# A fused attention and expert block on one core: three moves in the order of work on VectorE and ScalarE

## What is computed

```python
h = _layernorm(x) * (1 + ca) + sa
x = x + ga * attention(h)      # q, k = silu(h Wq), silu(h Wk); v, u = h Wv, h Wu
                               # kv_new = decay * kv + (k * k_decay)^T v, carried over the blocks
                               # o = q kv + masked (q k^T) v;  y = u * rms_normalised(o);  y Wout
h = _layernorm(x) * (1 + cb) + sb
out = (silu(h Wg_s^T) * (h Wu_s^T)) Wd_s^T               # shared expert
for e in range(8):
    out += (silu(h Wg[e]^T) * (h Wu[e]^T)) Wd[e]^T * comb[:, e]   # top 2 of 8
x = x + gb * out
```

## Time and profile before

| | us |
|---|---|
| median of the runs | 389.35 (389.18 to 389.91) |
| the profiled execution's own time | 391.22 |
| its span in the profile | 389.4 |
| busy PE / PE weight loads / DVE / ACT / POOL | 370.2 / 317.9 / 279.9 / 217.2 / 193.2 |
| mean granted clock of TensorE | 0.991 |

### The profile page before, as it was taken

How to read it: one execution, slowest core, us unless ns; L and a number is a source line. 1 busy time by engine, 2 the same in 40 slices (tenths; PEclk the granted TensorE clock), 3 DMA queues, 4 the chain that set the end, 5 groups by cost and what they waited for, 6 DMA issues and landing times.

```text
span 389.4 us, 12937 instructions
## 1 busy us (share of the span) xinstructions
PE 370.2 (95%) x4983; PEld 317.9 (82%) x4983; DVE 279.9 (72%) x561; ACT 217.2 (56%) x453; POOL 193.2 (50%) x193
## 2 busy tenths in 40 slices
PE   8989998999999888999995999999999999999996
PEld 4545555778877768899985999999999999999995
DVE  6986487898888786579983767758677785656553
ACT  5688676677667644648354655554646553433322
POOL 2000005787768665311373357686766665664340
PEclk9999999899999999999998999999999999999999
DMA  8952040000295006999432348564686776574543
GB/s 267 355 73 39 0 161 3 2 4 29 75 337 133 29 22 220 342 341 260 101 93 71 89 87 85 109 112 83 107 101 89 120 85 107 101 106 80 78 56 109
DMA packets 53043, 45.35 MB, mean 116 GB/s; under 512 B 31524, under 2 KB 46996, under 8 KB 52856
## 3 DMA queue, kind: packets, MB, share of 16 engines
q1 hardware_dynamic: 43048, 32.09, 29.9%
q0 software_dynamic: 7488, 10.27, 19.2%
q10 hardware_dynamic: 2448, 2.18, 1.8%
HBM read 27.60 MB, written 10.49 MB: 98 GB/s over the span
## 4 chain that ended last, share of the span: by engine, by line
PE 66%; POOL 12%; DVE 10%; issue 7%; ACT 3%; ACTq 0%; DVEq 0%; POOLq 0%
PE ps L1629 33%; PE ps L1647 16%; PE ps L1412 7%; POOL tmp L554 2%; POOL tmp L575 2%; POOL tmp L558 2%; POOL tmp L573 2%; POOL wx L563 2%; POOL h2s L579 2%; PE ps L1340 2%; DVE tmp L1253 1%; PE ps L1398 1%; PE ps L1532 1%; DVE tmp L1259 1%; PE ps L1509 1%
## 5 line engine op out<-in xcount | busy, mean ns | idle before, releaser
L1629 PE MATMUL ps<-tmp,wx 128*128 128x128 bf16 x1776 | 107.3, 220 | 5.2 <-ACT tmp L818 4.9
L1629 PEld LDWEIGHTS ps<-tmp,wx 128*128 (+1 forms) x1776 | 103.6, 99 | 6.5 <-ACT tmp L818 5.2
L611 POOL DMA_INDIRECT out<-tmp,dk x39 | 66.5, 1706 | 47.3 <-SPq L515 42.3
L856 ACT ACTIVATE tmp<-tmp 128x512 bf16<-128x512 f32 x55 | 34.6, 630 | 84.9 <-PE ps L1647 48.7
L1647 PE MATMUL ps<-wx,tmp 128*128 (+1 forms) x660 | 80.8, 273 | 0.3 <-DVE tmp L1259 0.2
L1253 DVE TENSOR_TENSOR tmp<-ps,tmp 128x512 f32<-128x512 f32 x55 | 37.9, 690 | 47.9 <-PE ps L1629 38.9
L1647 PEld LDWEIGHTS ps<-wx,tmp 128*128 128x128 bf16 x660 | 62.0, 98 | 7.8 <-issue 0.8
L1629 PE MATMUL ps<-w_hl,wx 128*128 128x128 bf16 x864 | 51.5, 219 | 1.0 <-ACT tmp L845 0.9
L1629 PEld LDWEIGHTS ps<-w_hl,wx 128*128 (+1 forms) x864 | 49.7, 98 | 1.7 <-issue 1.3
L606 POOL DMA_INDIRECT tmp<-h2rows,src_i x39 | 40.8, 1046 | 17.2 <-issue 10.7
L1259 DVE TENSOR_TENSOR tmp<-tmp 128x512 bf16<-128x512 f32 x55 | 37.8, 687 | 11.3 <-ACT tmp L856 10.8
(11 more groups left out here) (194 smaller groups left out, 569.1 us busy)
## 6 DMA issues: line engine op xcount, KB each, us to landing
wx<-in_wexp SPq DMA_DIRECT2D x26, 512.0 KB, 5.1
xres<-in_x SPq DMA_DIRECT2D x4, 512.0 KB, 7.2
h2rows<-h2s ACTq DMA_DIRECT2D x16, 128.0 KB, 4.0
out<-h2s SPq DMA_DIRECT2D x12, 128.0 KB
h2s<-in_wmod SPq DMA_DIRECT2D x1, 1024.0 KB, 9.4
wx<-decay_rows SPq DMA_DIRECT2D x16, 64.0 KB
modr<-mod_rows SPq DMA_DIRECT2D x1, 1024.0 KB, 4.7
wx<-in_wqkvu SPq DMA_DIRECT2D x1, 768.0 KB, 7.4
```

What stands on the lines that cost most here:

```text
L611: e.indirect_dma_start(t["out"], bass.IndirectOffsetOnAxis(ap=dst_i[:, j:j + 1], axis=0), yb[(NA + j) % 2], None, compute_op=ALU.add).then ...
L856: e.activation(hs[p][:, 0:FF], hf[p], ACT.Copy).then_inc(s["inner_high"], 1)
L1629: ins = e.matmul(half(bank, m * P), weight(at_, weights(part, w) + k * FF + m * P, P), xT[f % NXT][:, (2 * a + k) * P:(2 * a + k + 1) * P] ...
```

## The change

Three pieces of code stand in another place; nothing is added or taken away. In ACT's `middle(11)` the eviction `take_rows(12)` stands ahead of `split_high(1, 0)`. In DVE's prologue the low part of the weights' chunk 3 stands behind the moments of groups 2 and 3. In each attention step DVE makes the new state ahead of gating y.

```diff
@@ ACT, middle(f)
                     if f == EXP_AT:
                         softmax()
+                    if f == NA - 1:
+                        take_rows(NA)
                     for piece in PIECES_AT.get(f, ()):
                         split_high(*piece)
-                    if f == NA - 1:
-                        take_rows(NA)
                     wait(e, "inner_made", f + 1)
@@ DVE, prologue
             normalise(1)
-            weights_low(3)
             moments(2)
             moments(3)
+            weights_low(3)
             inputs_low(1)
@@ DVE, step_attention(n)
                 if mine(n) and n:
                     decay_scores(n)
-                if mine(v):
-                    _, b, i, j = tile_of(v)
-                    wait(e, "values_added", v + 1)
-                    wait(e, "squares", v + 1)
-                    wait(e, "out_product", v - 1)
-                    e.tensor_tensor(yfeat[:, v % 2], half(O_BANK, 0, D).rearrange("p (k n) -> p k n", k=KD),
-                                    ufeat[i // 2][:, i % 2, :, j * P:(j + 1) * P], ALU.mult).then_inc(s["y_gated"], 1)
                 if mine(n, NSTATE):
                     b = n % B
                     new = half(KT_BANK, D, D).rearrange("p (k n) -> p k n", k=KD)
                     wait(e, "kv_product", n + 1)
                     if n < B:
                         e.tensor_copy(state[:, b], new).then_inc(s["state_made"], 1)
                     else:
                         wait(e, "state_masked", n - 1)
                         wait(e, "state_decayed", KD * (n - 1))
                         e.tensor_tensor(state[:, b], state[:, b], new, ALU.add).then_inc(s["state_made"], 1)
+                if mine(v):
+                    _, b, i, j = tile_of(v)
+                    wait(e, "values_added", v + 1)
+                    wait(e, "squares", v + 1)
+                    wait(e, "out_product", v - 1)
+                    e.tensor_tensor(yfeat[:, v % 2], half(O_BANK, 0, D).rearrange("p (k n) -> p k n", k=KD),
+                                    ufeat[i // 2][:, i % 2, :, j * P:(j + 1) * P], ALU.mult).then_inc(s["y_gated"], 1)
```

## The result

| | median | runs | |
|---|---|---|---|
| before, same chip | 389.31 us | 4 (389.18 to 389.91) | |
| after | 381.12 us | 4 (380.34 to 381.49) | ratio 0.9781, 95% interval 0.9767 to 0.9796 |

The ratio times 389.3 is a gain of 8.5 us, with an interval of 7.9 to 9.1, and a time of 380.8 us beside the 389.35 that the prediction started from. The forecast was 382.1, the range 380.9 to 384.1: the gain is 1.2 us larger than forecast, and the time lies just under the range. The profiled execution of after took 380.34 us and has a span of 378.5; PE is busy for 364.9 us of it (96%).

A forecast was written before the change was run, and what follows sets the result against it. The prediction took PE, the busiest engine, as the bound, with its longest single wait at tile 12. Terms -6.46 - 0.5 - 0.33 = -7.3 us took the median from 389.35 to 382.1 us, range 380.9 to 384.1.

The forecast's parts named there:

- part 1, the hole: Tile 12: with the eviction ahead of the cast, PE starts at 203.44 instead of 208.48, gaining 5.04 us.
- part 1, the clock behind it: Tile 12: without the hole its 48 matmuls take 2.84 us instead of 4.26, gaining 1.42 us.
- part 2: Prologue: moving DVE's subtraction behind the moments lets ACT's root L666 start sooner, gaining 0.5 us.
- part 3, step 1: Attention step 1: PE's wait for the copy L1104 shortens, gaining 0.33 us once.
- part 3, steady steps: Twelve steady attention steps: idle time of 0.30 us moves from ahead of L1074 to ahead of L1080; gain 0.
- the two covers of 0.7 and 0.9 us: After tile 12's earlier start: room before PE waits for the third low part (0.7) and tile 11's low part (0.9).
- once more 1.4: Price if the clock stays low or falls elsewhere: again a half clock's cost here, 1.4 us, giving 383.5.
- the matmuls' low clock behind step 1's hole: Attention step 1: one of two reasons given for a time under 381.5, together given a chance of 0.03.
- The rival on the falling clock: Prologue's new hole or tile 12: the clock falls elsewhere or stays low, giving 383.5; chance 0.12.
- The prologue's new hole: Prologue, about 21.3 us: PE waits 0.95 us for the moved subtraction, covered by 1.14 us of existing idle time.
- the ring: Steady attention step: L1115, L773, L737 and L1080 wait on each other, setting 5.29 us whatever the swapped order.

The follow-up runs named there:

- e7: The kernel before, unchanged, run again for a second trace and twelve more times: 388.95 us, ratio 0.9991 against before.
- e13: The kernel before with 80 useless matmuls on PE ahead of the gate of tile 12, on a quiet chip: 387.19 us, ratio 0.9944.
- e5: The kernel before with 24 useless matmuls at the end of attention step 1 on PE, on a noisy chip: 391.27 us, ratio 0.9944.
- e9: The changed kernel with ACT's root L737 issued one place earlier, ahead of L773: 376.26 us, ratio 0.9656 against before.
- e2: The kernel before with only DVE's low part of chunk 3 moved behind the moments: 388.54 us, ratio 0.9972.
- e3: The kernel before with only DVE's new state moved ahead of gating y in the attention steps: 387.95 us, ratio 0.9955.
- e1: The kernel before with only ACT's eviction moved ahead of the cast: 382.46 us, ratio 0.9817.

## Why the prediction was right in kind and short in size

| step | predicted | found | from |
|---|---|---|---|
| part 1, the hole | -5.04 | -5.0 | starts of tile 12 in e7 and after: 206.37 - 200.82, less 0.56 of head start |
| part 1, the clock behind it | -1.42 | -2.2 | mean of four traces; e13 2.2 (1.4 to 3.0) |
| part 2 | -0.5 | -0.33 | PE's first attention rows, after against e7 (0.4 over all traces) |
| part 3, step 1 | -0.33 | -0.24 | 0.33 less 0.1 that L1080's wait gives back |
| part 3, clock of step 1 | not in the sum | -0.8, worked out | 16 of 28 executions x 1.35 us |
| part 3, steady steps | 0 | 0 | 80.87 us over the row of L1080s in before and after |
| sum | -7.3 | -8.6 | measured -8.5 (-9.1 to -7.9) |

**Part 1** stood as argued: the eviction needs only the turned rows and ACT's turn, PE's hole went whole, the two covers of 0.7 and 0.9 us held, and ACT and DVE caught up in two tiles. The first step that failed is "The 48 matmuls took 4.26 us there and 2.84 at 213.88: 1.42 us lost". It took a single execution's loss for the loss; the runs put it at 2.2 us. That execution was the cheapest of the four traced, one episode where the others had two: 1.42 against 2.11, 2.40 and 2.77, the hole being the same. The bound that I gave a half clock, "once more 1.4", was for the rivals upwards; nothing in the range stood for the clock costing more before, and so gaining more now.

**Step 1's clock** is the second step that failed, a term that the sum put at nothing: "the matmuls' low clock behind step 1's hole" was in the 0.03 for less than 381.5, and some 0.8 us in its place is what traces and counts give. The row that would have priced it, 0.57 in 68 to 72 us, was in the trace, next to rows 6. The mean clock told of it too, where the prediction took its 0.991 as a sign against a swinging clock: 0.009 of 389.4 us is 3.5 us of clock missing, tile 12's window holds 0.34 x 4.3 = 1.5 of them, and 68 to 72 us holds 0.43 x 4.0 = 1.7. I priced the clock where the wait table showed its longest entry, and did not go down the clock column over the whole span. The two clock terms are 0.8 us each above what I had; parts 2 and 3 gave 0.26 less. That makes 1.3 us, against 1.2 missing. That the shorter hole ends the episodes rests on counts, 16 of 28 against 0 of 20, and on e5, where useless work in the same hole did the same.

**The rival on the falling clock** had it at the wrong place and with the wrong sign. The prologue's new hole of 1.07 us cost no clock: it is in after, whose nine executions all have 0.999 or 1.0. The Trainium skill, "TensorE: Matmul & The Clock Gate", section "A second HAM failure mode: psum-queue depth-cycling", which I held against this change, has many small idle times make the clock swing. In this kernel the clock fell in the attention's first steps in some executions before the change, behind one hole of 1.90 us, and no longer did with the hole at 1.57; whether what the page tells of is at work here no run shows. Its outcome here, 383.5, did not come.

**Part 2** was read rightly in place and hole, and is a little smaller than 0.5. Its run alone gave 0.7 to 1.5, more than the move of 0.3 to 0.4 us that the traces show; a part of that is the baseline (against the 36 executions it is 0.7), the rest is clock, or open.

**Part 3** at nothing in the steady steps is the best supported of all: 80.87 us over the row of L1080s in before and in after, the plain step of 5.29 in every trace of that order, and e9, in which the wait ahead of L1080 goes as soon as the ring is opened. A plain step falls by no more than 0.08 us there, since PE comes next; the three steps with a cast inside the ring show it more plainly, 18.69 to 14.33. The cover of this zero was what the prediction named, L1115 and L773 and L737 and L1080 in a ring.

**The sum's baseline.** The profiled execution of before took 391.22 us, more than any of the 56 later ones of that kernel on the quiet chips (at most 390.33). Its span is 10.9 us longer than that of after, of which 1.8 us are in the routed tiles (from tile 13 at 213.88 to an L1647 at 370.10, 156.2 us, where e7 takes 154.4, from 213.12 to 367.50), only 0.5 of them shown as idle time of PE, and 0.94 the start-up, which differs between executions of any of these kernels (the first warm-up matmuls, L1340, take 5.38 us in e7, 5.68 in e2, 6.79 in e3 and 6.83 in e1). Taking its difference from the median off, as the prediction did, kept both out of the sum. What made the routed tiles slower is open.

## What to carry to other kernels

Price a hole of PE with the clock behind it, and take that price from several executions: the mean clock of each run counts the low stretches even where there is one trace. Check that the parts, run alone, add up to the whole; here they made 10.0 for 8.5, and a second set of runs of the unchanged kernel showed how much of that was the baseline. Before swapping two instructions to shorten a loop, write down the ring that sets its step; a swap gives nothing if both stand ahead of the same member, and moving one member out of the ring (here a 0.24 us root that a 1.04 us cast had got in front of in three steps) gave 4.3 us. Work that only frees a buffer or prepares a later tile belongs behind everything that PE waits for in this one.

## What was not expected of the hardware

- The same hole does not cost the same. Behind 4.90 us of idleness of PE the low clock took 1.42 us in one execution and 2.77 in another of the same kernel, and behind 1.90 us of idleness it came in 16 of 28 executions and cost 1.15 to 1.46 us in the three traces in which it was timed.
- Useless matmuls buy the clock back: 80 of them in the hole of tile 12 took 2.2 us (1.4 to 3.0) off, and tile 12 started no earlier. Removing the hole is better by its length, 5.0 us.
- A swing of 0.33 us in a hole's length (1.90 to 1.57) went with the end of the low clock behind it. Why is not shown.
- One chip gave the kernel before 390.0 to 395.8 us where the timed runs on the others gave 388.5 to 390.3; ratios taken there have intervals 0.5 to 0.8% wide, in place of 0.2 to 0.4%, and two of the four came out lower than the parts explain.
